# Self-attention lead-in: heads side by side in the first head pair's query scores, dense half steps one per unit, the second half's values copied by ScalarE and biased by GpSimd

## What is computed

```python
x_norm = modulate(_ln(x), shift_a, scale_a)
qkv = x_norm @ W_qkv + b_qkv
q, k, v = jnp.split(qkv, 3, axis=-1)
...
attn_w = jax.nn.softmax(jnp.einsum('bhqd,bhkd->bhqk', q, k) * scale, axis=-1)
attn_out = jnp.einsum('bhqk,bhkd->bhqd', attn_w, v)
```

## Time and profile before

| | |
|---|---|
| median of 3 runs | 1573.97 us |
| the runs | 1573.97, 1571.93, 1583.33 us |
| the profiled execution | 1573.0 us |
| its span, first to last instruction | 1571.2 us |
| around the span | 1.8 us |
| mean granted TensorE clock | 0.978 |
| busy: TensorE, VectorE, ScalarE, GpSimd | 1452.7, 1052.8, 767.8, 395.9 us |

### The profile page before, as it was taken

How to read it: one execution, slowest core, us unless ns; L and a number is a source line. 1 busy time by engine, 2 the same in 40 slices (tenths; PEclk the granted TensorE clock), 3 DMA queues, 4 the chain that set the end, 5 groups by cost and what they waited for, 6 DMA issues and landing times.

```text
span 1571.2 us, 26548 instructions
## 1 busy us (share of the span) xinstructions
PE 1452.7 (92%) x10495; PEld 915.3 (58%) x10495; DVE 1052.8 (67%) x2994; ACT 767.8 (49%) x1248; POOL 395.9 (25%) x447
## 2 busy tenths in 40 slices
PE   5889999999999999978998999999999999997898
PEld 3447674344455857656774767444445585765676
DVE  2584356899847446799547544799983754679953
ACT  1335422788844533335552643288884453332554
POOL 4420015642125100113215000664202510001320
PEclk9899998899999999999999999999999999999999
DMA  9500024221020000000040000632102000000000
GB/s 339 174 1 1 0 83 94 42 43 22 2 81 1 1 1 3 2 1 1 1 165 11 1 1 0 165 53 42 22 2 81 1 1 0 3 2 1 1 1 27
DMA packets 41503, 57.86 MB, mean 37 GB/s; under 512 B 10915, under 2 KB 30659, under 8 KB 40603
## 3 DMA queue, kind: packets, MB, share of 16 engines
q1 hardware_dynamic: 25239, 34.71, 6.8%
q0 software_dynamic: 13360, 14.09, 5.1%
q10 hardware_dynamic: 2780, 7.36, 1.3%
HBM read 40.26 MB, written 2.10 MB: 27 GB/s over the span
## 4 chain that ended last, share of the span: by engine, by line
PE 66%; DVE 25%; ACT 4%; issue 2%; DMA 2%; POOL 1%; ACTq 0%; DVEq 0%
PE ps L1039 9%; PE ps L1053 8%; PE ps L488 6%; PE ps L1398 4%; PE ps L898 4%; PE ps L1189 3%; DVE taken L2478 3%; DVE rs L2148 3%; DVE taken L2490 2%; PE ps L876 2%; PE ps L1423 2%; PE ps L1180 2%; PE ps L624 2%; DVE mxw L2140 2%; PE ps L1024 2%
## 5 line engine op out<-in xcount | busy, mean ns | idle before, releaser
L1715 ACT ACTIVATE pt<-ps 128x512 f32<-128x512 f32 x512 | 274.5, 596 | 66.4 <-PE ps L1039 50.7
L2341 DVE TENSOR_REDUCE mm<-ps 128x1 f32<-128x1024 f32 x240 | 288.6, 1222 | 23.3 <-PE ps L1024 20.8
L2596 POOL TENSOR_TENSOR rstd<-ve,minus_half 128x4 f32<-128x4 f32 x32 | 35.0, 1095 | 615.3 <-DVE ve L2012 615.3
L1039 PE MATMUL ps<-qx,kx 50*128 50x512 f32 x512 | 187.8, 457 | 0.8 <-ACT pt L1715 0.8
L1024 PE MATMUL ps<-kx,qx 48*128 48x512 f32 x480 | 180.2, 456 | 1.2 <-DVE mm L2341 1.1
L1053 PE MATMUL ps<-pt,v 128*32 128x256 f32 x2048 | 158.4, 394 | 0.1
L1039 PEld LDWEIGHTS ps<-qx,kx 50*128 50x128 f32 x512 | 79.8, 188 | 88.5 <-ACT pt L1715 69.9
L2225 DVE TENSOR_TENSOR rlo<-ring,rhi 128x512 fp32r<-128x512 f32 x48 | 33.2, 691 | 91.9 <-ACT ring L1667 91.9
L1053 PEld LDWEIGHTS ps<-pt,v 128*32 128x32 f32 x2048 | 44.4, 109 | 84.2 <-ACT pt L1715 56.7
L2643 POOL DMA_DIRECT2D qx<-mxT x64 | 35.9, 563 | 195.7 <-ACT mxT L1709 165.0
L616 PE MATMUL ps<-filler 128*128 128x512 f32 x256 | 83.1, 456 | 0.0
(11 more groups left out here) (378 smaller groups left out, 3380.7 us busy)
## 6 DMA issues: line engine op xcount, KB each, us to landing
wm<-in_L_xcond_W_mlp_dram SPq DMA_DIRECT2D x4, 1024.0 KB, 8.2
w3a<-in_L_xcond_w_m_dram SPq DMA_DIRECT2D x2, 2048.0 KB, 9.0
qx<-q_hi POOLq DMA_DIRECT2D x56, 64.0 KB, 2.3
kx<-k_hi POOLq DMA_DIRECT2D x56, 64.0 KB, 2.3
w<-in_L_xcond_e_w_dram SPq DMA_DIRECT2D x6, 512.0 KB, 7.5
w<-in_L_xcond_e_w_dram SPq DMA_DIRECT2D x2, 1536.0 KB, 13.6
s_ada<-in_L_xcond_w_ada_dram ACTq DMA_DIRECT2D x1, 2304.0 KB, 23.7
w3b<-in_L_xcond_w_m_dram SPq DMA_DIRECT2D x2, 1024.0 KB, 11.3
```

Of the source, the lines that this page charges most:

```text
L1039: pe.matmul(ps[:, bank, :], kx[r, p % 4, kc * P:(kc + 1) * P], qx[r, p % 4, half * 512:(half + 1) * 512], start=True, stop=True).then_inc( ...
L1715: act.activation(pt[:, n % 8, i * 512:(i + 1) * 512], ps[:, bank, :], ACT.Exp, scale=QK_SCALE).then_inc(st_read, 1)
L2341: return dve.tensor_reduce(mm[:, p % 2, e, t:t + 1], place().rearrange("p a q -> p (a q)"), X, ALU.max).then_inc(ring_read, 1)
```

## The change

- *Heads side by side.* All 16 query units of head pair 0 have one product per head, on the two row halves; VectorE's maxima of all 16 go to `mmq`, and the second group of maxima gets the extra small operation (the maximum over the two key halves) too.
- *Half steps.* The values' tiles of the second half come as one contraction step per unit (units 0 to 5), `full_step` as one half per unit (6, 8 to 12; unit 7 has two). The last two full parts, for tokens 512 to 1023, now use banks 7 and 6, and the gates' products banks 4 and 5. `full` gets another layout in `hT`, which GpSimd's split reads.
- *Fillers.* Two in unit 13 and two in each of the key units 0 to 3. Those of the units 11 and 12 and the five before key unit 0 are gone; before, 11 to 13 had two each, and key units 0 to 3 one.
- *Values of the second half.* ScalarE copies them from PSUM in two operations; GpSimd adds the bias in SBUF after `spread(2)`; the first product that reads them (w = 2) waits for it.
- *Turn of the first maxima.* At the start of unit 9 in place of its end; the bank order of `key_bank` is shifted by two, so that the turn uses bank 6. `full_step(6)` waits for ScalarE's copy of it. Key unit 1 waits for the last full part, the fillers of unit 13 for the last but one.

```diff
@@ -106,7 +106,9 @@
 k = n - TAIL_KEY
-return 4 + n % 3 if k < 0 else (4 + TAIL_KEY % 3, 4 + (TAIL_KEY + 1) % 3, 4 + (TAIL_KEY + 2) % 3, 1, 3)[k % 5]
+spare = [4 + (TAIL_KEY + i + 2) % 3 for i in range(3)] + [1, 3]
+return 4 + (n + 2) % 3 if k < 0 else spare[k % 5]
@@ -955,27 +957,27 @@
-def values(k, tiles=range(TB)):
+def values(k, tiles=range(TB), steps=range(KC)):
...
     for t in tiles:
-        for c in range(KC):
+        for c in steps:
             ins = pe.matmul(ps[:, 2 + 2 * k + t // 2, t % 2 * D:(t % 2 + 1) * D], hT[:, k, c, t * P:(t + 1) * P],
                             wv2[:, c, :], start=c == 0, stop=c == KC - 1)
-    if tiles[-1] == TB - 1:
+    if tiles[-1] == TB - 1 and steps[-1] == KC - 1:
         ins.then_inc(v_done, 1)
...
 residual(1, 1)
-pe.wait_ge(v_ready, b * NB + 1)
+pe.wait_ge(v_ready, b * 3 + 1)
 linear(2, wqk2, KC, hT[:, 0]).then_inc(full_done, 1)
...
     qk, k, c = j // 2 % 2, j // 4, j % 2
-    ins = pe.matmul(ps[:, (7, 6, 7, 5)[j // 2], cols], wqk2[:, c, (qk * KC + 1) * P:(qk * KC + 2) * P], hT[:, k, c, cols],
+    ins = pe.matmul(ps[:, (7, 6, 7, 6)[j // 2], cols], wqk2[:, c, (qk * KC + 1) * P:(qk * KC + 2) * P], hT[:, k, c, cols],
                     start=c == 0 and cols.start == 0, stop=c == KC - 1 and cols.stop == BLK)
@@ -1012,9 +1014,9 @@
 bank = take()
-if p == 0 and u < T:
+if p == 0:
     for e in range(2):
-        r, t, half = slice(64 * e, 64 * e + 3 * HD), u % TB, u // TB
+        r, t, half = slice(64 * e, 64 * e + 3 * HD), u // T * TB + u % TB, u % T // TB
         ins = pe.matmul(ps[:, bank + e, :], qx[r, 0, t * P:(t + 1) * P], kx[r, 0, half * 512:(half + 1) * 512],
@@ -1044,6 +1046,8 @@
 pe.wait_ge(st_read, b * N_KEY + entry_of[2 * w + 1])
+if w == 2 and i == 0:
+    pe.wait_ge(v_ready, b * 3 + 3)
 if kc == 0 and half == 0 and p >= 1:
@@ -1076,54 +1080,60 @@
     if n == 0:
-        keep_busy(5, 5)
         pe.wait_ge(gates_ready, b + 1)
+    elif n == 1:
+        pe.wait_ge(full_ready, b * 4 + 4)
     elif n == 6 * T:
...
     key_scores(p, u, 0)
-if m == 11:
-    pe.wait_ge(full_ready, b * 4 + 4)
-if m >= 11 and n < 4:
-    keep_busy(5 if n < 0 else 7, 2 if n < 0 else 1)
 if m == 0:
...
     pe.wait_ge(spread_ld[0], b * (first + 2 * N_SPR) + first)
+elif m == 9:
+    pe.wait_ge(full_ready, b * 4 + 2)
+    turn_maxima(0, 0)
 elif at_m == 0:
...
 query_scores(q, at_m)
-if m < TB - 1:
-    values(1, (m + 1,))
-elif m == 3:
+left, right = slice(0, 2 * P), slice(2 * P, BLK)
+if m < 6:
+    values(1, (1 + m // 2,), (m % 2,))
+elif m == 6:
     pe.wait_ge(full_ready, b * 4 + 1)
-    full_step(4, slice(0, 2 * P))
-elif m == 4:
-    full_step(4, slice(2 * P, BLK))
-    full_step(5, slice(0, 2 * P))
-elif m == 5:
-    full_step(5, slice(2 * P, BLK))
-elif m == 6:
-    pe.wait_ge(v_ready, b * NB + NB)
-    full_step(6)
+    full_step(4, left)
 elif m == 7:
-    full_step(7, slice(0, 2 * P))
+    full_step(4, right)
+    full_step(5, left)
 elif m == 8:
-    full_step(7, slice(2 * P, BLK))
+    full_step(5, right)
+elif m == 9:
+    pe.wait_ge(st_read, b * N_KEY + 1)
+    full_step(6, left)
 elif m == 10:
-    pe.wait_ge(full_ready, b * 4 + 3)
+    full_step(6, right)
+elif m == 11:
+    full_step(7, left)
+    pe.wait_ge(v_ready, b * 3 + 2)
     for j in range(3):
         o = N_ROW * b + R_G_A + j
-        ins = pe.matmul(ps[:, 7 - j // 2, j % 2 * D:(j % 2 + 1) * D], row_of[:, o:o + 1].broadcast_to([P, P]), row_hl[:, :], start=True, stop=True)
+        ins = pe.matmul(ps[:, 4 + j // 2, j % 2 * D:(j % 2 + 1) * D], row_of[:, o:o + 1].broadcast_to([P, P]), row_hl[:, :], start=True, stop=True)
     ins.then_inc(gates_spread, 1)
+elif m == 12:
+    full_step(7, right)
+elif m == 13:
+    pe.wait_ge(full_ready, b * 4 + 3)
 if n >= 0:
     key_scores(p, u, 1)
+if 13 <= m and n < 4:
+    keep_busy(7, 2)
 for i in bursts_of(n):
     weigh_values(i // 2, i % 2)
-if at_m == 9 and q < NP:
+if at_m == 9 and 1 <= q < NP:
     turn_maxima(q, 0)
@@ -1722,7 +1732,7 @@
 col = (C_BQ2, C_BK2)[qk] + 1
-affine(full[qk][:, k * BLK:(k + 1) * BLK], ps[:, bank, :], 1.0, colT[:, col:col + 1]).then_inc(full_ready, 1)
+affine(full[qk][:, k, :], ps[:, bank, :], 1.0, colT[:, col:col + 1]).then_inc(full_ready, 1)
@@ -1730,15 +1740,20 @@
 full_part(0, 0, 7)
-act.wait_ge(full_done, b * 6 + 5)
-full_part(0, 1, 7)
-act.wait_ge(full_done, b * 6 + 6)
 full_part(1, 0, 6)
-full_part(1, 1, 5)
+act.wait_ge(v_done, b * NB + NB)
+act.wait_ge(v2_clear, b + 1)
+for j in range(2):
+    ins = act.activation(v2[:, TB + 2 * j:TB + 2 * j + 2, 0:H * VS].rearrange("p t (h d) -> p t h d", d=VS)[:, :, :, 0:HD],
+                         ps[:, 4 + j, :].rearrange("p (t h d) -> p t h d", t=2, d=HD), ACT.Copy)
+ins.then_inc(v_ready, 1)
 maximum_rows(0)
 act.wait_ge(gates_spread, b + 1)
-act.activation(gates[:, 0:2, :], ps[:, 7, :].rearrange("p (j n) -> p j n", j=2), ACT.Copy)
-act.activation(gates[:, 2, :], ps[:, 6, 0:D], ACT.Copy).then_inc(gates_ready, 1)
+act.activation(gates[:, 0:2, :], ps[:, 4, :].rearrange("p (j n) -> p j n", j=2), ACT.Copy)
+act.activation(gates[:, 2, :], ps[:, 5, 0:D], ACT.Copy).then_inc(gates_ready, 1)
+act.wait_ge(full_done, b * 6 + 6)
+full_part(0, 1, 7)
+full_part(1, 1, 6)
 scored = 2
@@ -2334,8 +2349,8 @@
 def query_maximum(p, u):
-    if p == 0 and u < T:
-        dst = mmq[:, u // TB, :, u % TB]
+    if p == 0:
+        dst = mmq[:, u % T // TB, :, u % TB]
         return dve.tensor_reduce(dst, place(), X, ALU.max).then_inc(ring_read, 1)
@@ -2344,7 +2359,7 @@
 top = mm[:, p % 2, :, half * TB:(half + 1) * TB]
-if p == 0 and half == 0:
+if p == 0:
     link(dve.tensor_tensor(top, mmq[:, 0, :, :], mmq[:, 1, :, :], ALU.max))
@@ -2369,8 +2384,6 @@
 query_maximum(q, at_m)
-if m == TB - 1:
-    add_v2(1)
 if at_m % T == T - 1:
@@ -2679,6 +2692,9 @@
     spread(2)
+    pool.wait_ge(v_ready, b * 3 + 2)
+    v_in = v2[:, TB:T, 0:H * VS].rearrange("p t (h d) -> p t h d", d=VS)[:, :, :, 0:HD]
+    pool.tensor_tensor(v_in, v_in, vb2[:, :].rearrange("p (h d) -> p h d", d=HD).unsqueeze(1).broadcast_to([P, TB, H, HD]), ALU.add).then_inc(v_ready, 1)
 elif p == 1:
```

8 lines of the change are left out of this document (4 added, 4 removed).

## The result

| | before | after |
|---|---|---|
| median | 1573.46 us (4 runs, 1571.93 to 1583.33) | 1555.53 us (4 runs, 1554.23 to 1555.66) |
| profiled execution, its span | 1573.0, 1571.2 us | 1555.66, 1553.8 us |
| mean granted clock | 0.978 | 0.985 |

The ratio is 0.9864, with a 95% interval from 0.9821 to 0.9906. In spans the change gave 1571.2 - 1553.8 = 17.4 us. Forecast were 11.1 (one fall of the clock) + 5.0 (2.5 for each of the two elements) = 16.1.

A forecast was written before the change was run, and what follows sets the result against it. TensorE held 66% of the chain, with VectorE pacing the lead-in. 1573.0 - 11.1 (one clock fall) - 2 x 2.5 = 1556.9; with half of the median's 0.97 carried over, 1557.5 us, range 1553 to 1569 (forecast's own 1554 to 1561).

The forecast's parts named there:

- The clock: Self-attention lead-in: the granted clock falls in neither element after the change, -11.1 us in element 0.
- the late fall: Rival: one element's clock still falls late in the lead-in, as now; 1566 to 1571 us, chance 0.10.
- the early one: Rival: less dense units make the clock fall early; one element 1575 us (0.04), both 1580 to 1598 (0.06).
- First key product: End of the lead-in: the first key product starts 16.4 us after the first pair, 3.7 earlier than 20.1.
- One filler more each, 0.23, so 1.54 a unit ... 0.9 is lost: Key units n = 0 to 3, TensorE the bound: one more filler each, 4 x 0.23 = 0.9 us lost per element.
- the 0.3 for three products on a row half: n = 0 and 1: side-by-side heads share a row half with both key products; 0.15 us a unit, 0.3 in all.
- The pace: Lead-in query units: VectorE's maxima set the pace at 1.15 us, TensorE's pair and half step taking 1.06.
- The table load: ScalarE's Exp table load (1.28 us) comes after the full parts, ending at 17.6; first key scores are ready at 16.9.
- cost 0: First Exp 0.7 us late behind the table load; ScalarE catches up by n = 2, three key banks cover it.
- The copies and GpSimd's addition: Second half's values: ScalarE copies 0.6 to 0.7 us each, GpSimd's addition done at 20.5, hidden with 7 us to spare.
- The median: Baseline: timed median 1573.97 us is 0.97 above the profiled 1573.0; half is carried over, giving 1557.5.

The follow-up runs named there:

- the filled kernel before: The kernel before with two 512-column fillers more behind each of query units 8, 9 and 10: 1564.51 us, ratio 0.9976.
- the bunched one: The changed kernel with dense steps bunched as before (two value steps in units 0 to 2, full_step in 3 to 8, none from 9): 1574.68 us, ratio 1.0047.
- the filled variant: The changed kernel with the bias addition back on VectorE and four fillers ahead of the turn in unit 9: 1556.59 us, ratio 0.997.
- the late addition: The changed kernel with GpSimd's bias addition waiting for VectorE's three small operations behind unit 15's maximum: 1555.35 us, ratio 0.9962.

## Why the prediction was right in its mechanism, and which step failed

*The clock: right, and shown.* The fall of element 0 is gone, and it was worth the 11.1 us read from the difference of the two elements. That there was one to remove in each of the four timed executions of the kernel before was luck: in the later sessions most had none, and against those the attention gains only 3.2 us an element. The forecast's reason (each unit keeps a step of 128 rows) is what the filled kernel before and the bunched one bear out, from both sides. Two of its rivals, the late fall and the early one, did not come. But the forecast had missed how near a fall still was: with the addition left on VectorE the same dense steps did not hold the clock in 9 of 12 executions. That part of the change was priced only by its 1.28 us, and by the times of that variant it was worth more. That its worth lies in the wait ahead of the turn is argued, not shown.

*First key product: 3.7 forecast, 3.4 measured* (20.12 - 16.73). It came at 16.73, not at 16.4. The parts add up: the addition 1.1 (from the filled variant), the pairs on two row halves 0.9 (from units 8 to 15 on one half), leaving 1.4 for the five fillers, the 1.37 of the earlier trace rows; this last is the remainder of a sum, not a run. The forecast's 16.4 was too early by 0.3 already at the last half step, which ended 15.3 after the first pair and not 14.8; the full parts and fillers behind it took 1.4 in place of 1.6.

*The step that failed: "One filler more each, 0.23, so 1.54 a unit ... 0.9 is lost", and the 0.3 for three products on a row half.* Together a loss of 1.2 us; the runs showed 0.18. From the first key product to that of n = 4 it is 5.87 (1010.34 - 1004.47), against 5.69 before (1027.72 - 1022.03). The first key products of n = 1 to 4 of the kernel before, element 1:

```profile
1023.46 0.39 PE L1039 MATMUL ps<-qx,kx 50*128 50x512 f32 x1
...
1024.78 0.40 PE L1039 MATMUL ps<-qx,kx 50*128 50x512 f32 x1
...
1026.10 0.40 PE L1039 MATMUL ps<-qx,kx 50*128 50x512 f32 x1
...
1027.72 0.50 PE L1039 MATMUL ps<-qx,kx 50*128 50x512 f32 x1
```

They lie 1.43, 1.32, 1.32 and 1.62 apart with one filler each, where now 1.55, 1.56, 1.32 and 1.44 hold two. I had added the second filler's length to the distance of before, as if the products around it stayed as they were. But the fillers were also moved, from between the key product and the query pair to behind the unit, and that let four products run two by two. By the rule above a distance of before, at n = 1 and 2, is 0.89 + 0.43 for one filler = 1.32, and one of after, at n = 2, 0.66 + 0.66 for two fillers = 1.32. (The 1.31 that the forecast read as the distance of all four is that of n = 1 and 2 alone; the sum took only what was added to it, so this did not enter.) For n = 0 and 1 three products on one half did cost 0.22 each, the upper bound and not the 0.15 that I took. So it is 3.39 - 0.18 = 3.2 an element in place of 2.5, and that is the 1.3 us by which 17.4 exceeds 16.1.

*The pace: right in its end, wrong in its maker.* The maxima stand back to back at 1.14, but the pairs with one half step follow each other at TensorE's 1.06. In the lead-in TensorE's products wait for VectorE for more than 0.1 only ahead of the turn (0.34 and 0.36). So VectorE's first eight maxima set the time of the turn, and from there TensorE's steps and ScalarE's full part (0.35 of wait ahead of the fillers) that of the first key product. The forecast had VectorE pace the units up to the last half step. The two runs that moved it agree: the addition on VectorE, ahead of the turn, made it 1.1 later, and 0.23 more in four of TensorE's pairs behind the turn 0.9.

*The table load: the trace decides.* In the changed kernel's row the load of 1.28 ends at 261.04 and the first Exp starts at 261.05, with its scores out since some 0.7 us (259.88 + 0.50). So there is no drain behind the load here. By the Trainium skill (ScalarE: Activation LUTs, "What ACT_TABLE_LOAD costs") some 1.38 us more would have followed; this case does not show them. My "cost 0" for the late first Exp was right for the kernel as changed, and wrong as soon as n = 1 became shorter.

*The copies and GpSimd's addition: right.* 0.55 each for the strided copies; the addition was done at 264.1, and the first product that reads its result started at 271.6. The small operation beside it took 0.65, at a cost of 0.1 us an element at most, since the late addition gave no more back.

*The median.* I set the time against one of 1573.97, and against the profiled run with one fall. It is a mixture: later sessions had medians of 1562.94, 1564.64 and 1560.89 for the same kernel. The forecast of the changed kernel's own time was hardly touched by this, since the changed kernel hardly varies: 1555.5, 1554.2. But what the change is worth as a ratio depends on how many executions of the kernel before have a fall. What decides that, the chip, the session or the execution, stays open; no run here was made for it.

## What to carry to other kernels

Where two batch elements run the same instructions and one is slower, compare their granted clocks first: here that difference was worth more than all the instructions moved. Put dense 128-row steps evenly between narrow products, and ask of each wait of TensorE there whether it makes a hole; that a hole lets the clock fall is likely from the runs here, not shown. Run two variants that are to be told apart by a fall in the same session, since the same kernel had falls in 14 of 35 executions in one and in 1 of 19 in another. When a filler or a dense product is moved, look at which products then stand next to each other and on which row half, before adding its length.
